# Edge pass of a graph network: two scratch rows of GpSimd are left out of each step

## The reference

```
src, dst = edge_index                      # dst sorted, both below 6250
gate = silu(edge_attr @ F1W + F1b) @ F2W + F2b
ei, ej = emb[atom_z[src]], emb[atom_z[dst]]
gate = gate + (ei * (ej @ adapt)).sum(-1, keepdims=True)
cw = where(distances < 6, 0.5 * (cos(pi * distances / 6) + 1), 0)
mj = node_mult[dst]
msg = gate * h[dst] * (cw * mj)[:, None]
agg = segment_sum(msg, src)                # over all edges of a source node
tot = clip(segment_sum(mj, src), 1e-8)
h = layernorm(h + agg / tot)
# then four rounds of attention over the same edges, with segment softmax
```

## Time and profile before

| | |
|---|---|
| median of two runs | 19803.65 us |
| profiled execution, first to last instruction | 20537.4 us (no other time is recorded for it) |
| GpSimd busy in it | 10469.6 us, 51% |
| gathers of the edge pass, first start to last start | 2632.9 to 6894.8 us |
| gathers there, mean of one | 1088 ns, 1820 in the window 2640 to 6900 us |
| iotas there, mean of one | 982 ns, 455 in that window |
| GpSimd busy in that window | 3029.66 of 4260 us |

### The profile page before, as it was taken

The page is one execution under the profiler, slowest core; times in us unless marked ns, Lnnn a source line. Parts: engine busy times, 40 slices in busy tenths (PEclk is TensorE's granted clock), DMA queues, the critical chain, the costliest instruction groups (busy, mean ns, idle before and its releaser), DMA issues. The chain is left out here.

```text
span 20537.4 us, 413891 instructions
## 1 busy us (share of the span) xinstructions
PE 10575.6 (51%) x122618; PEld 8403.7 (41%) x122618; DVE 11669.1 (57%) x28337; ACT 4919.9 (24%) x14465; POOL 10469.6 (51%) x11911
## 2 busy tenths in 40 slices
PE   1000055656666647865884787488424444334333
PEld 1000033333333236855884686478423333233233
DVE  4045155556555756873886588378623333357758
ACT  0000022222222114433442443244212222210110
POOL 5677766777777303421441343144167777674370
PEclk9995555555555569987996899699767777655556
DMA  8997554444444435435442543444311111134334
GB/s 59 90 175 155 62 65 62 65 63 67 64 64 65 74 100 155 123 77 165 123 123 68 174 123 98 133 133 122 80 41 46 47 44 48 37 113 137 114 112 133
DMA packets 2671466, 1951.72 MB, mean 95 GB/s; under 512 B 787834, under 2 KB 2449042, under 8 KB 2670285
## 3 DMA queue, kind: packets, MB, share of 16 engines
q1 hardware_dynamic: 1922578, 1150.35, 23.5%
q0 software_dynamic: 309216, 536.66, 15.2%
q10 hardware_dynamic: 439512, 262.80, 6.5%
HBM read 1287.52 MB, written 723.39 MB: 98 GB/s over the span
## 5 line engine op out<-in xcount | busy, mean ns | idle before, releaser
L594 POOL DMA_INDIRECT edges_rows<-raw,edges_perm_now x1824 | 1984.0, 1088 | 1008.3 <-issue 512.4
L594 POOL DMA_INDIRECT attend_rows<-key_rows,attend_fetch_now x1824 | 1837.0, 1007 | 1048.8 <-POOL attend_fetch_now L1587 726.8
L594 POOL DMA_INDIRECT keys_rows<-table,keys_staged x1564 | 1679.4, 1074 | 533.7 <-issue 474.2
L594 POOL DMA_INDIRECT mlp_xin<-table,mlp_staged x1564 | 1519.9, 972 | 757.6 <-POOL mlp_idle L629 399.4
L1652 PE MATMUL attend_seg<-attend_rows,attend_hot 128*128 128x49 f32 x14592 | 1807.7, 278 | 68.6 <-issue 46.1
L1652 PEld LDWEIGHTS attend_seg<-attend_rows,attend_hot 128*128 128x128 f32 x14592 | 1720.0, 194 | 100.2 <-issue 79.7
L1707 DVE TENSOR_REDUCE attend_mraw<-attend_top 128x2 f32<-128x1024 f32 x912 | 1114.8, 1222 | 522.9 <-remote 283.3
L1032 PE MATMUL edges_ps_t<-ident,edges_attr 128*40 128x128 f32 x1824 | 426.3, 413 | 1912.0 <-ACT edges_attr L1087 1742.0
L600 POOL DMA_INDIRECT messages<-spread_out,spread_place_now x912 | 1201.9, 1318 | 394.0 <-issue 341.9
L1462 POOL COPY expand_table<-k 128x156 bf16 x912 | 291.5, 320 | 1811.7 <-PEq L1476 738.9
L2379 PE MATMUL spread_ps<-spread_table,spread_oht 128*128 128x48 bf16 x10944 | 561.3, 214 | 1221.2 <-DVE spread_msg L2395 408.7
(11 more groups left out here) (513 smaller groups left out, 29327.4 us busy)
## 6 DMA issues: line engine op xcount, KB each, us to landing
key_rows<-expand_out ACTq DMA_DIRECT2D x304, 624.0 KB
attend_ea<-edge_attrs SPq DMA_DIRECT2D x912, 160.0 KB
tally_rows<-messages SPq DMA_DIRECT2D x152, 864.0 KB, 4.8
expand_oht<-dst_hots SPq DMA_DIRECT2D x304, 384.0 KB, 3.5
attend_oht<-src_hots SPq DMA_DIRECT2D x912, 128.0 KB
attend_lane_hot<-src_hots_by_edge SPq DMA_DIRECT2D x912, 128.0 KB
raw<-keys_rows ACTq DMA_DIRECT2D x46, 1445.0 KB
messages<-keys_zeros SPq DMA_DIRECT2D x171, 384.0 KB
```

The lines of the kernel that those rows point to most:

```text
L594: return nc.gpsimd.indirect_dma_start(out=out, out_offset=None, in_=table, in_offset=bass.IndirectOffsetOnAxis(ap=index, axis=0))
```

## The change

`edge_pass` no longer declares the tile `idle` and the semaphore `s_idle`, and GpSimd no longer calls `rest_pool` ahead of columns 3 and 6, so that the 8 gathers of a step follow each other. `rest_pool` itself stays, and the MLP pass calls it as before.

```diff
         perm_now = ph.sb("perm_now", [P, TURN, COL], I32)
-        idle, s_idle = ph.sb("idle", [P, REST]), ph.sem("s_idle")
         place_now = ph.sb("place_now", [P, TURN, CHR], I32)
...
                     pool.sem_inc(s_pool_turn, 1)
                     for c in range(COL):
-                        if c in (3, 6):
-                            rest_pool(g, pool, idle, s_idle, n * 2 + c // 3, s_pool_turn)
                         gather(nc, rows[b][:, c, :], k.raw, perm_now[:, b, c:c + 1]).then_inc(s_rows[b], 16)
```

## The result

The changed kernel took 19197.81 us (median of two runs, 19172.42 and 19223.19) against 19803.65 us: ratio 0.969, 95% interval 0.965 to 0.973, 606 us less. The prediction was 19250 us, a saving of 554 us. The sum and its mechanism hold for the chips on which the kernel before takes about 19850 us. They do not hold everywhere: on another chip of the same type the same change cost 0.6%, and most of what follows is about that.

A forecast was written before the change was run, and what follows sets the result against it. The prediction took GpSimd's instruction stream, with its iotas and their waits, to bound the edge pass. 681 us saved, less 57 for VectorE and 70 for pauses, gave 554 us: about 19250 us, range 19090 to 19600.

The forecast's parts named there:

- The sum: Whole kernel: 681 - 57 - 70 = 554 us saved, a step of about 16.3 us, about 19250 us.
- GpSimd's stream as the bound: Edge pass: GpSimd's instructions set the pace; without iotas and their waits 681 us less, 2.98 us a step.
- over 3700: Sign in the changed profile: edge-pass gathers from first to last over 3700 us instead of 4262.
- The two parts: Edge pass: the 456 iotas' own length, 448 us, and the longer gaps behind them, 233 us; sum 681 us.
- VectorE against GpSimd: Edge pass: VectorE's instructions meet gathers and scatters more often without iotas and lengthen them, giving back 57 us.
- The three long meetings a step: Edge pass: three port conflicts with VectorE, 2.5 us each, cost 7.4 us a step against 2.98 saved; kernel near 20800 us.
- Pauses: Edge pass: late TensorE results show through more as the buffer cushion shrinks; GpSimd's 33.6 us of waiting trebles, 70 us lost.
- The first, the loop of the other engines: Edge pass: loop of ScalarE, TensorE and VectorE becomes the bound at 16.5 us plus 0.6 a step; 19440 us, chance 0.14.
- The third: Edge pass: iotas pace gathers; without them an outstanding-transfer limit holds each step's fourth to eighth gather; 20235 us, chance 0.05.

The follow-up runs named there:

- kind B: Not an edit: chips on which the kernel before the change takes about 20570 us; the unchanged changed kernel measured 20707 us there, ratio 1.0061.
- kind A: Not an edit: chips on which the kernel before the change takes about 19850 us; the result's runs, ratio 0.969, are of this kind.
- the third one: The changed kernel timed and profiled once more with no edit, beside the kernel before at 19889 us: 19318 us, ratio 0.971.

## Why the prediction was right, and where

**Where luck came in.** The prediction was worked out from a profile of kind B, and its result was timed on kind A, where it is right. For the chips from which its own rows come it would have been wrong: there the change made the kernel 0.6% slower. Nothing in its reasoning chose between the two.

**GpSimd's stream as the bound, 681 us.** Right on kind A: 15.65 us a step against 15.7 by the account. The profile gave 3568 us for the pass, below the "over 3700" of the forecast, as the 57 and 70 us below hardly showed. The two parts were checked apart on kind B, where with both iotas GpSimd's stream still is most of the bound: the wait 219 us of 233, the length of the iota 251 us of 368, the rest of it going into late signals.

**VectorE against GpSimd, 57 us.** Not confirmed. The gathers average 1.086 us, as before (1.088), where 1.11 to 1.13 was forecast. The scatters are longer, 1.206 against 1.084 us, 456 x 0.122 = 55 us, which is the size forecast in another place; but this sets a trace of kind A against one of kind B. Within one kind the scatters did not grow: 1.084 to 1.011 us on B, and on A 1.197 us with one short iota against 1.206 and 1.200 without. So no run shows the 57 us as a cost of the change. The three long meetings a step that the prediction worked out from the Trainium skill (SBUF — State Buffer, section "SBUF: two separate sides"), and that would have put the kernel near 20800 us, are not in the trace: the longest gather is 2.02 us. VectorE's L1139, the former L1142, takes at most 0.47 us, where it was 1.53, as forecast.

**Pauses, 70 us.** On kind A too large: GpSimd waited 12 us for the rows-seen signal in the result's trace and 38 us in the third one. On kind B far too small: its gathers waited 520 us for it, and 650 us for ScalarE. This is the weak step of the prediction, at the sentence that lets ScalarE's gate wait 622.4 us with no releaser on record and prices only what shows through of it. I took these pauses as given and asked only how well four buffers hide them. But they depend on the change: on kind B VectorE stood idle for the lookups' signals for 308 us in sum with the iotas and for 1664 us without.

**The sum.** 681 - 57 - 70 = 554 us, against 606 and 571 us measured on kind A. The 681 us alone are above both, so 75 to 110 us were given back there. No kernel before was profiled on kind A, so what they are isn't known, and that the two small terms add up to about as much is no proof of either. TensorE's clock stayed at its lower level, 0.50, in the pass after, at 74% busy.

**Taking a profile and a median together.** The 3.6% between span and median was noted and left. It was the mark that they come from different conditions, and the attention's gathers, at 6717 us, would have been no help before the result, as nothing stood beside them.

**The rivals.** The first, the loop of the other engines, came true on kind B, at 19.1 us a step and not the 17.1 that I priced: I took its pace from VectorE's and ScalarE's own steps, while it is made of the unbroken stream plus some 5.4 us, by the one step read above. The third named the right property, pacing, and the wrong sufferer: the gathers run faster without the pauses (1.029 us), and TensorE's signals suffer.

**Not settled.** By what path GpSimd's issues hold back a signal of TensorE, and what differs between the two kinds of chip, or between the places on a chip at which the program ran. Whether it is the issuing itself or the gathers' transfers that hold them back isn't separated. That the signals come late while GpSimd issues without a break is shown by their records and by how their number changes over five kernels on kind B; that they then set the pace of the pass is the reading of one step and of the kernel without scatters. Why runs of three gathers hold up signals in the edge pass and none in the MLP pass isn't known. That it is the pause as such that lets them through, and not the iota, is only argued: the 0.175 us iota with its wait did no worse than the 0.98 us one, but every pause tried on kind B held an iota, and the waits for landed rows ran on kind A only.

## What to carry to other kernels

An instruction that computes nothing may help by breaking a stream: before it is taken out, look for waits on another engine that have no releaser on record, and ask whether they come while the stream runs. If the span of a profile and the median of the runs differ by more than the runs do among themselves, compare a phase that nothing touches before any number of one is set against the other. A saving of 3% that rests on one chip wants a second one. And a count that rests on recorded rises is checked against how long the receiver stood idle, as rises can be missing.

## What the runs showed of the hardware

The same program took 19889 us on one chip and 20564 to 20573 us on three others, each within 0.4% of its median there; from the first to the last gather of the attention it is 6162 to 6216 us in the four profiles of one kind and 6717 to 6828 us in the ten of the other. On the second kind the signal of TensorE's lookups reached VectorE a median 8.47 us behind the modelled end of the matmul when GpSimd issued the DMAs of a step without a break, and 1.38 us with an iota after every third gather; on the first kind it was 0.01 us without any iota. In the MLP pass of the second kind, with three gathers between iotas, no receiver waited over 0.5 us past a modelled end; with 34 gathers in a row 230 of 1656 waited over 1 us.
